# One query-score tile and its maximum moved earlier within each head step of a latent-attention layer

## The reference

```
latent = x @ Wkv_down                       # 64 numbers per token
q, k, v = x @ Wq, latent @ Wk_up, latent @ Wv_up      # 16 heads of 64
attn = softmax(where(causal, q k^T / 8, -inf))        # 16 heads, 512 x 512
x = x + (attn @ v) @ Wout
```

## Time and profile before

| | |
|---|---|
| median of 3 runs | 3108.84 us |
| lowest, highest | 3107.92, 3110.38 us |
| the profiled execution: its own time | 3109.72 us |
| the profiled execution: span | 3108.0 us |
| mean granted TensorE clock | 0.908 of full speed |
| latent-attention stage with values (batches 0 to 7) | about 2035 to 2835 us of the span |

### The profile page before, as it was taken

One profiled execution on the slowest core, in us unless ns is written; L12 is line 12 of the kernel. 1 busy time (PEld: TensorE's weight loads), 2 busy tenths in 40 slices (PEclk: granted clock), 3 DMA queues, 4 the chain that ended last, 5 costly groups with the idle time before them and its releaser, 6 DMA issues. The chain is left out here.

```text
span 3108.0 us, 38743 instructions
## 1 busy us (share of the span) xinstructions
PE 2517.6 (81%) x13889; PEld 1339.3 (43%) x13889; DVE 2180.1 (70%) x3910; ACT 1427.3 (46%) x2061; POOL 842.7 (27%) x820
## 2 busy tenths in 40 slices
PE   7967999899998999989678256688888888886256
PEld 3423444344443444444333134345555555554134
DVE  3597776757858688576970765488888878973765
ACT  5533354444544445444234111167667766774111
POOL 3323354443443444434133000002112211212000
PEclk9988999999999999999889578599999999998578
DMA  5000000000000000000000100000000000000101
GB/s 167 12 0 1 1 1 1 1 1 1 1 1 1 1 1 1 1 1 1 1 1 18 42 1 27 9 1 2 2 2 3 2 3 1 2 2 14 47 0 55
DMA packets 29460, 33.08 MB, mean 11 GB/s; under 512 B 6568, under 2 KB 25704, under 8 KB 29272
## 3 DMA queue, kind: packets, MB, share of 16 engines
q1 hardware_dynamic: 28296, 28.02, 2.9%
q0 software_dynamic: 976, 2.56, 0.3%
HBM read 25.72 MB, written 4.19 MB: 10 GB/s over the span
## 5 line engine op out<-in xcount | busy, mean ns | idle before, releaser
L661 POOL TENSOR_TENSOR g_lo<-g_full,g_hi 128x512 f16<-128x512 f32 x512 | 660.5, 1292 | 1024.6 <-ACT g_hi L727 1019.3
L727 ACT ACTIVATE g_full<-hid,b_col 128x512 f32<-128x512 f32 x512 | 352.7, 689 | 627.6 <-PE hid L152 625.9
L150 PE MATMUL acc<-g_hi,w_hi 128*128 128x512 f16 x1024 | 394.4, 385 | 58.2 <-POOL g_lo L661 58.2
L150 PE MATMUL hid<-y_hi,w_hi 128*128 128x512 f16 x1024 | 396.2, 387 | 25.0 <-DVE y_lo L715 20.9
L151 PE MATMUL acc<-g_lo,w_hi 128*128 128x512 f16 x1024 | 395.1, 386 | 0.0
L152 PE MATMUL acc<-g_hi,w_lo 128*128 128x512 f16 x1024 | 394.9, 386 | 0.0
L151 PE MATMUL hid<-y_lo,w_hi 128*128 128x512 f16 x1024 | 394.9, 386 | 0.0
L152 PE MATMUL hid<-y_hi,w_lo 128*128 128x512 f16 x1024 | 394.0, 385 | 0.0
L727 ACT ACTIVATE g_hi<-hid,b_col 128x512 f16<-128x512 f32 x512 | 350.0, 684 | 0.0
L1975 DVE TENSOR_REDUCE mla_m_col<-mla_ps 128x1 f32<-128x512 f32 (+3 forms) x512 | 224.9, 483 | 60.4 <-PE mla_ps L1817 54.7
L2078 ACT ACTIVATE mla_p_full<-mla_ps 128x1280 f32<-128x1280 f32 x128 | 158.4, 1237 | 138.9 <-PE mla_ps L1847 138.5
(11 more groups left out here) (368 smaller groups left out, 4737.1 us busy)
## 6 DMA issues: line engine op xcount, KB each, us to landing
stage<-in_L_ffn_w_dram SPq DMA_DIRECT2D x16, 512.0 KB, 5.0
x<-in_L_attn_x_dram SPq DMA_DIRECT2D x8, 512.0 KB, 8.6
routed_w<-in_L_ffn_w_dram SPq DMA_DIRECT2D x4, 1024.0 KB, 8.1
out_dram<-x SPq DMA_DIRECT2D x8, 512.0 KB, 5.7
mla_sums<-mla_sum_row SPq DMA_DIRECT2D x128, 2.0 KB
mla_wq<-in_L_attn_Wq_dram SPq DMA_DIRECT2D x1, 1024.0 KB, 7.4
mla_wout<-in_L_attn_Wout_dram SPq DMA_DIRECT2D x1, 1024.0 KB, 9.7
routed_wqkv<-in_L_ffn_wq_dram SPq DMA_DIRECT2D x2, 256.0 KB, 3.6
```

Of the source, the lines that this page charges most:

```text
L150: pe.matmul(out, w_hi, v_hi, start=first, stop=False)
L661: pool.tensor_tensor(g_lo[:, g, :], g_full[:, g, :], g_hi[:, g, :], ALU.subtract).then_inc(tail_done, 1)
L727: act.activation(out[:, g, :], hid[:, ht % 4, :], ACT.Gelu, bias=b1_col[:, ht:ht + 1], scale=1.0 / WS).then_inc(gelu_done, 1)
```

## The change

In TensorE's step, QSlast goes from behind PV to directly behind ST, so ahead of OUT, SPR, the transposes and PV. In VectorE's step, the maximum of tile 1 goes from behind all the pieces of that step to directly behind the other three maxima. No instruction is added or removed; no DMA and no other engine's order is touched.

```diff
@@ tensor_step
                 last.then_inc(st_done, 1)
+            hb, hh, hn = head_of(b, h + LEAD - 2)
+            if exists(hb):
+                pe.wait_ge(s_max, TILES * hn + 1)
+                query_scores(pe, (slot + (h + LEAD - 2) // H) % 2, hh, QUERY_TILES[-1]).then_inc(s_rest, 1)
             if exists(before) and OUTPUT_AT <= h < OUTPUT_AT + TILES:
...
                 last.then_inc(pv_done, 1)
-            hb, hh, hn = head_of(b, h + LEAD - 2)
-            if exists(hb):
-                pe.wait_ge(s_max, TILES * hn + 1)
-                query_scores(pe, (slot + (h + LEAD - 2) // H) % 2, hh, QUERY_TILES[-1]).then_inc(s_rest, 1)
@@ vector_step
                 for t in QUERY_TILES[:-1]:
                     query_maxima(dve, hh, t)
+                dve.wait_ge(s_rest, hn + 1)
+                query_maxima(dve, hh, QUERY_TILES[-1])
...
-            hb, hh, hn = head_of(b, h + LEAD - 2)
-            if exists(hb):
-                dve.wait_ge(s_rest, hn + 1)
-                query_maxima(dve, hh, QUERY_TILES[-1])
             hb, hh, hn = head_of(b, h + 1)
```

## The result

The changed kernel takes 3147.4 us (median of 4 runs, 3146.58 to 3147.47) against 3109.6 us for the kernel before on the same chip: a ratio of 1.0122, 95% interval 1.0104 to 1.0139. It is slower by 37.8 us; the forecast was 3141, slower by 32.8, in a range of 3121 to 3156. The profiled execution has a span of 3144.9 us, 36.9 more than before.

A forecast was written before the change was run, and what follows sets the result against it. The prediction took TensorE and VectorE, both near full, to bound the stage, neither alone. Output steps 20.9, batch 0 4.1 and spread steps 7.8 gave +32.8 us on the 3108.84 median, so 3141; range 3121 to 3156.

The forecast's parts named there:

- the new wait: TensorE ahead of OUT in step 13: waits for tile 3's maximum; new pause 1.75 us, next QS3 1.06 us later.
- Steps 11 to 15: Losses of 1.62, 1.06 and 0.81 us in steps 11, 13 and 15; 3.49 us together, +20.9 us over batches 1 to 6.
- Steps 12 and 14: Even steps with OUT: tile 3's maximum is there before ST ends, so nothing is added, 0.
- Batch 0: No OUT or SPR there; odd steps 1, 3, 11, 13, 15 lose 0.81 us each, +4.1 us.
- Spread steps 3 to 10: Batches 1 to 7: late TensorE partly hidden; +0.28 us per pair of steps, +7.8 us in all, bounds -8 and +22.
- the four pairs: Pairs of spread steps followed through one by one gave 0.27, 0.3, 0.4 and 0.1 us; +0.28 was taken.
- against it: Spread steps: VectorE's pieces of the next batch no longer delay QS3, set against the losses; no separate size given.
- The clock: New TensorE pauses of 1.75 and 2.31 us in steps 13 and 11: no clock loss taken; otherwise 1.7 us per stretch.
- rival 1: The clock falls too: one half-clock stretch in each of six batches gives +10 us, 3151; two, 3161. Chance 0.10.
- the pause that cost nothing: Batch 4 of the kernel before: a 1.73 us pause, with the batch running at 1.00 of full clock.
- Rival 2: VectorE hides losses in batch 0 and spread steps: 3130; if step 15's loss is hidden too, 3125. Chance 0.19.
- Rival 3: Faster: tile 3's maximum is there when ST ends, saving 0.69 us per odd output step; 3100, 8 us gained. Chance 0.05.

The follow-up runs named there:

- the filled kernel: Changed kernel with six overwritten 512-column matmuls ahead of the new wait in every odd step: 3118.6 us, ratio 1.0029 to the kernel before.
- the run with OUT steps only: Kernel before with the new order in steps 11 to 14 alone, all other steps as before: 3138.3 us, ratio 1.0093.
- the even-steps run: Kernel before with the new order in even steps alone, odd steps as before: 3114.6 us, ratio 1.0014.
- the run with TensorE's half alone: Kernel before with QSlast moved as in the changed kernel, VectorE's maximum of tile 1 left where it was: 3149.9 us, ratio 1.0125.
- tile 3 first: Changed kernel with tile 3's maximum moved ahead of the four query instructions in steps 10, 12 and 14: 3118.7 us, ratio 1.0029 to the kernel before.
- the last tile behind OUT: Kernel before with QSlast behind OUT, ahead of PV, in steps 11 to 14, its maximum directly behind the other three: 3103.3 us, ratio 0.9979.
- the control: Kernel before, own order, with six overwritten 512-column matmuls ahead of QS3 in step 1: 3107.6 us, ratio 0.9990.

## Why the prediction was right, and where its terms were off

**What bounds it, and the new wait.** Right. TensorE waits for tile 3's maximum behind ST, in odd steps, because VectorE has the query instructions first. In step 13 the new pause was to be 1.75 us and OUT to start 1.91 behind ST's end. It was 1.74 (2438.11 to 2439.85; the row says 1.58, as it counts from ST's last result) and 1.91 (2438.11 to 2440.02). QS3 came 1.07 later (forecast 1.06).

**Steps 11 to 15.** Forecast +3.49 us a batch, +20.9 in sum. By `p_lo`, steps 11 to 0 measured 3.54, in six batches 21.2, in the changed kernel, and 3.52 in the filled one. `p_lo` has its own place in the step, and so splits the batch a little differently from TensorE. From ST to ST, both kernels lose 1.31 in step 11, 1.06 in step 13 and 0.83 in step 15 (batch 1), 3.20 in sum. Steps 13 and 15 are as forecast. Step 11 was put 0.31 too high: its 1.62 holds with the old order up to step 10, as the run with OUT steps only shows, and not with the new one.

**Steps 12 and 14.** Forecast 0. Right in the changed kernel (0.0 from ST to ST); the even-steps run shows that this held only with the odd steps moved too.

**Batch 0.** Forecast +4.1. In the filled kernel, where no half-clock stretch falls into it, `p_lo` moved by 3.25 us from head 1 of batch 0 to head 1 of batch 1, which includes step 15. The size is right, somewhat high. The steps ahead of batch 0 were left out of the forecast, though QSlast moves in them too: from the stage's first maximum to its first `p_lo` the kernel before takes 29.25 us, the changed and the filled kernel 30.98 and 31.00. That is a term of +1.7 put at nothing.

**Spread steps 3 to 10.** Forecast +7.8 us, bounds -8 and +22. Here the step "nearer to what the four pairs give when followed through one by one" failed. The clean figure is the filled kernel's: -1.06 us a batch for steps 2 to 10, -6.4 in six batches, and about +1 in batch 7, once the stretch that the kernel before has there is taken out. That is -5.4, near the lower bound. What I had as "against it", that VectorE's pieces no longer delay QS3, outweighed TensorE's wait: the gains are in steps 2, 6, 8 and 10 (-0.44, -0.40, -0.59, -0.45), three of which have a group's maxima to evict, and one the latent. The query copies do wait longer, as I said of step 6 (45.5 us in the filled kernel, 13.5 before), but VectorE's wait for QSlast fell by more (51.4 to 6.9), and the run with TensorE's half alone has this gain turned into a loss. A whole batch was to be about 4.6 us longer; in the filled kernel it is 3.52 - 1.06 = 2.46 (3.20 - 0.74 from ST to ST). I did not take these steps apart further.

**The clock.** Forecast 0, with rival 1 at a chance of 0.10 and 1.7 us a stretch. This was the second term mis-sized. I took the new pauses to be "nearer to the pause that cost nothing", and looked for stretches behind step 11 only. The price was right: 1.65 us each. The count was not: 17 against 6, ten of them with the pauses of steps 5 and 7, 1.9 to 2.4 us long, which I had not priced at all; only one followed step 11, where I had looked. The filled run makes it a measured term: 11 more stretches x 1.65 = 18.2 us of the 37.8. The Trainium skill (TensorE: Matmul & The Clock Gate, the section on psum-queue depth-cycling) says that frequent short pauses between groups of matmuls can make the clock swing between half and full. I set this aside on the strength of one batch; the trace agrees with it, with 17 stretches, and with 18 us instead of the 10 that I had given to it.

**The sum.** The change without the clock: the last `p_lo` of the filled kernel is 11.5 us late, with 5 stretches fewer than the kernel before, so 11.5 + 5 x 1.65 = 19.7. With 18.2 for the clock that is 37.9, and the changed kernel's last `p_lo` is 38.0 us late. The 19.7 are 0.9 us by which this run was late when the stage began, 1.75 ahead of batch 0, 3.25 in batch 0, 6 x 2.46 = 14.8 in batches 1 to 6, 1.0 in batch 7, and -1.9 behind the turns of the loop at batches 3 and 5, which no run explains. So about half of the loss is order and half is clock. My 32.8 had the output steps nearly right, the spread steps 13 us too high and the clock 18 us too low. That two errors of opposite sign nearly cancelled is luck, and the reason why the total came out so near.

**The rivals.** Rival 1 (clock) was true besides the forecast, not instead of it. Rival 2 (VectorE hides more) was near in its number for the spread steps, but not in its reason: they gained, by VectorE's moved maximum. Rival 3 (faster) named the right condition, that tile 3's maximum be there at ST's end: tile 3 first, and the last tile behind OUT, each bring that about, and the second is faster than the kernel before.

## What to carry to other kernels

Before a wait is moved ahead of work that did not need it, follow the awaited instruction back on its own engine: what stands in front of it there is the price. Look for the place where some work covers the wait and other work covers its successor; here it was between OUT and PV, one group further down. And where an edit makes pauses on TensorE, price the half-clock stretches as a term of their own, since they can cost as much as the pauses; filling a pause with matmuls that nobody reads separates the two in one run.

## What I had not expected of the hardware

- Half-clock stretches followed pauses of 1.98 and 2.42 us, but not every such pause. In the changed kernel, step 5 has a pause of 2.42 us in batches 1 to 7, with a stretch in batches 1, 3, 4 and 6 alone; step 9 has one of 2.63 in batches 1 to 6, with a stretch in batches 3 and 5 alone. So the length of a pause did not decide by itself. In the kernel before, the clearest case was a pause of 3.10, and batch 4 had a pause of 1.73 with no stretch behind it. Still, the control removed stretches behind such pauses in batches 1, 2 and 6: one undisturbed batch says little of the others.
- Each stretch of 3.4 us at half clock moved the following step by 1.65 us, nearly all of the 1.7 that it takes from TensorE; little was hidden, though VectorE is about as busy.
- Six more matmuls in each odd step (366 over the run), read by nobody, made the changed kernel 28.8 us faster.
